# Turning the gated rows with VectorE and on-chip DMAs instead of TensorE in a Mamba-2 plus MoE-LoRA block

## The reference, cut to what matters

```python
g = y * jax.nn.silu(gate)                       # [tokens, 8192]
gg = g.reshape(b, s, G, INTER // G)             # 8 groups of 1024 channels
var = jnp.mean(gg * gg, axis=-1, keepdims=True)
gg = gg * jax.lax.rsqrt(var + EPS)
out = gg.reshape(b, s, INTER) * norm_w
return jnp.einsum('bsi,oi->bso', out, out_proj_w)   # [tokens, 512]
```

## Time and profile before

| what | value |
|---|---|
| time, median of 3 runs | 1656.18 us (1655.62 to 1657.89) |
| the profiled execution: time | 1656.76 us |
| the profiled execution: span of the trace | 1654.6 us |
| PE busy | 1616.8 us, 98% |
| DVE busy | 1367.3 us, 83% |
| POOL busy | 1341.1 us, 81% |
| ACT busy | 1232.1 us, 74% |
| granted TensorE clock, mean | 0.999 |

### The profile page before, as it was taken

How to read it: one execution, slowest core, us unless ns; L and a number is a source line. 1 busy time by engine, 2 the same in 40 slices (tenths; PEclk the granted TensorE clock), 3 DMA queues, 4 the chain that set the end, 5 groups by cost and what they waited for, 6 DMA issues and landing times.

```text
span 1654.6 us, 31655 instructions
## 1 busy us (share of the span) xinstructions
PE 1616.8 (98%) x10792; PEld 1300.1 (79%) x10792; DVE 1367.3 (83%) x1675; ACT 1232.1 (74%) x2625; POOL 1341.1 (81%) x1238
## 2 busy tenths in 40 slices
PE   7999999999999999999999999999999999999998
PEld 6777878878787877878778787887878787787776
DVE  5979788887979878788888888888788887879787
ACT  5267787777877777777877778687786877778775
POOL 3148689886998779897798968988698977989797
PEclk9999999999999999999999999999999999999999
DMA  3253366553644545454554535535454365544463
GB/s 129 68 190 112 101 186 178 152 155 109 197 127 123 151 154 163 112 149 128 166 176 116 157 115 166 164 115 164 125 183 125 115 170 141 158 127 146 127 164 104
DMA packets 216399, 236.09 MB, mean 143 GB/s; under 512 B 154280, under 2 KB 155824, under 8 KB 212016
## 3 DMA queue, kind: packets, MB, share of 16 engines
q1 hardware_dynamic: 216240, 234.08, 47.7%
HBM read 147.52 MB, written 55.05 MB: 122 GB/s over the span
## 4 chain that ended last, share of the span: by engine, by line
PE 65%; POOL 13%; ACT 8%; DVE 7%; issue 6%; DMA 0%; ACTq 0%; DVEq 0%; POOLq 0%; SPq 0%
PE P L261 8%; PE P L263 8%; PE P L262 8%; PE P L470 5%; PE P L480 5%; PE P L345 4%; PE P L487 4%; PE P L339 4%; PE P L338 4%; PE P L481 4%; ACT P L583 4%; PE P L495 3%; DVE hsX L790 2%; POOL xch L1115 2%; POOL AL L1090 2%
## 5 line engine op out<-in xcount | busy, mean ns | idle before, releaser
L583 ACT ACTIVATE P<-AB,SC 128x128 f32<-128x128 f32 x1016 | 305.9, 364 | 0.0
L261 PE MATMUL P<-xh,AH 128*128 128x512 f32 x656 | 267.8, 408 | 2.6 <-DVE xl L891 1.8
L790 DVE SCALAR_TENSOR_TENSOR hsX<-P,cwt,hsX 128x1023 f32<-128x1023 f32 x189 | 241.9, 1280 | 25.7 <-ACT hsX L520 21.2
L263 PE MATMUL P<-xh,AL 128*128 128x512 f32 x656 | 257.1, 392 | 0.0
L262 PE MATMUL P<-xl,AH 128*128 128x512 f32 x656 | 255.5, 389 | 0.0
L755 ACT ACTIVATE sq<-yb 128x512 bf16<-128x512 f32 x128 | 80.8, 631 | 212.6 <-DVE yb L1054 212.6
L1090 POOL TENSOR_TENSOR AL<-AR,AH 128x512 fp32r<-128x512 f32 x82 | 116.1, 1416 | 133.5 <-ACT AH L507 133.4
L480 PE MATMUL P<-OH,gTh 128*128 128x512 f32 x512 | 214.6, 419 | 2.5 <-DVE hsX L1070 1.5
L338 PE MATMUL P<-GH,xh 128*128 128x512 f32 x512 | 200.1, 391 | 0.2 <-ACT GH L552 0.2
L481 PE MATMUL P<-OH,gTl 128*128 128x512 f32 x512 | 200.3, 391 | 0.0
L339 PE MATMUL P<-GH,xl 128*128 128x512 f32 x512 | 199.6, 390 | 0.0
(11 more groups left out here) (214 smaller groups left out, 4144.2 us busy)
## 6 DMA issues: line engine op xcount, KB each, us to landing
AB<-acr_d SPq DMA_DIRECT2D x128, 512.0 KB, 4.6
half_d<-hsX SPq DMA_DIRECT2D x60, 512.0 KB, 3.3
AR<-in_wa SPq DMA_DIRECT2D x80, 256.0 KB, 2.8
TS<-in_wg SPq DMA_DIRECT2D x16, 1024.0 KB, 5.8
TS<-in_wo SPq DMA_DIRECT2D x16, 1024.0 KB, 4.8
part_d<-pl SPq DMA_DIRECT2D x64, 256.0 KB, 3.1
pl<-part_d SPq DMA_DIRECT2D x64, 256.0 KB, 3.2
SC<-sct_d SPq DMA_DIRECT2D x16, 128.0 KB, 5.3
```

What stands on the lines that cost most here:

```text
L261: te.matmul(o, ah_, bh_, start=(first and i == 0), stop=False)
L263: r = te.matmul(o, al_, bh_, start=False, stop=(last and i == n - 1))
L583: r = se.activation(decays(m)[:, h, :], AB[m % 2][:, h, :], ACT.Relu, bias=SC[s % 2][:, c, 3, h:h + 1], scale=-1.0)
L790: ve.scalar_tensor_tensor(out=o[:, d:T], in0=raw[:, 0:T - d], scalar=cwt[:, n, 3 - d:4 - d], in1=o[:, d:T], op0=ALU.mult, op1=ALU.add).the ...
```

## The change

The four PE transposes of each slot go (except in the last slot, which keeps them: `by_pe(j)` is true for `j == M - 1`). In their place:

- DVE turns the gated rows in 32x32 blocks with one `transpose` instruction (128x512) right after the gating, into a tile `blk`. It reads `yb` with a stride of 16 elements.
- SP moves the four bands of 32 partitions with four plain SBUF-to-SBUF DMAs (64 KB each) into `GTd[j % 2]`, a tile of 128 partitions. Partition `q` then holds channel `4q + k` in its part `k`; the host lays out the output weights and the norm weights to suit.
- ACT's `gTh` and DVE's `gTl` read `GTd` in SBUF, no longer bank 6 in PSUM. They are made one slot later, and the output product `O(j)` runs in slot `j + 2` instead of `j + 1` (`out_slot`); the products of slots 126 and 127 both come after slot 127.
- All that hangs on `O` moves one slot with it: ACT's copy or scaling of partial sums, DVE's alo, POOL's addition, SP's stores and loads. The splitting of the output weights moves from chunk 0 to chunk 1 on ACT (`OH`, except in segment 0) and for POOL's `OL`, and from chunk 1 to chunk 2 on DVE (`OL`); the next gate weights are loaded in chunk 3.
- Two groups of semaphores used in the preparation are merged to make room for the new ones.

```diff
+    def by_pe(j):
+        return j == M - 1
+
+    def out_slot(j):
+        return j + 1 if by_pe(j) else j + 2
+
+    outs_of = {m: [j for j in range(M) if out_slot(j) == m] for m in range(M + 2)}
...
-        if m:
-            jobs += [("O", m - 1, (4,))]
+        jobs += [("O", j, (4,)) for j in outs_of[m]]
...
-        if m < M:
+        if m < M and by_pe(m):
             jobs += [("GTr", m, (6,))]
...
+        gtd = sb("gtd", [128, 512])
...
+        blk, GTd = al[0], [al[1][:, :], gtd[:, :]]
...
+        def turned_rows(j):
+            if by_pe(j):
+                return bank("GTr", j).rearrange("p (k a i) -> p k a i", k=4, a=4)
+            return GTd[j % 2].rearrange("p (a k i) -> p k a i", a=4, k=4)
...
+                for j in outs_of[m + 1]:
+                    if by_pe(j):
+                        se.wait_ge(s_gtr, 1)
+                    else:
+                        se.wait_ge(gate_in[j % 2], 64 * (j // 2 + 1))
+                    if j:
+                        se.wait_ge(s_o, j)
+                    se.activation(by_block(gTh), turned_rows(j), ACT.Copy).then_inc(s_gth, 1)
...
-                    if c == 0:
+                    if c == (1 if s else 0):
                         se.wait_ge(s_ts3, s + 1)
                         se.wait_ge(ts_in, 16 * (3 + 2 * s))
...
-                    if c == 1:
+                    if c == out_c:
                         dve_output_lo(s, (1, 2))
...
                     ve.tensor_tensor(yb[:, :], bank("Y", m), tg[:, :], ALU.mult).then_inc(s_g, 1)
+                    if not by_pe(m):
+                        ve.wait_ge(s_g, m + 1)
+                        if m:
+                            ve.wait_ge(gate_in[(m - 1) % 2], 64 * ((m - 1) // 2 + 1))
+                        ve.transpose(blk[:, :].rearrange("p (b i) -> p b i", i=32),
+                                     yb[:, :].rearrange("p (j b) -> p b j", b=16)).then_inc(s_blk, 1)
...
-                if m < M:
-                    ve.wait_ge(s_gth, m + 1)
-                    ve.tensor_tensor(gTl[:, :, :], bank("GTr", m).rearrange("p (k t) -> p k t", k=4),
-                                     as_f(gTh[:, :, :]), ALU.subtract).then_inc(s_gtl, 1)
+                for j in outs_of[m + 1]:
+                    ve.wait_ge(s_gth, j + 1)
+                    ve.tensor_tensor(by_block(gTl), turned_rows(j), as_f(by_block(gTh)), ALU.subtract).then_inc(s_gtl, 1)
...
+        def sp_turn_rows(j):
+            sp.wait_ge(s_blk, j + 1)
+            if j >= 2:
+                sp.wait_ge(s_gtl, j - 1)
+            for a in range(4):
+                sp.dma_start(GTd[j % 2][:, a * 128:(a + 1) * 128], blk[32 * a:32 * a + 32, :]).then_inc(gate_in[j % 2], 16)
...
+                if m and not by_pe(m - 1):
+                    sp_turn_rows(m - 1)
```

147 lines of the change are left out of this document (81 added, 66 removed).

## The result

The changed kernel takes 1721.01 us (median of 4 runs, 1715.95 to 1727.43) against 1656.51 us (1655.62 to 1657.89) for the kernel before on the same chip: a ratio of 1.0391, 95% interval 1.0345 to 1.0436. It is slower by 64 us. The forecast was 1651 us, with a range from 1620 to 1684.

A forecast was written before the change was run, and what follows sets the result against it. PE, busy 98% of the span, was taken to pace the kernel; head -3, seven periods -10.5, last slots +5 and end +3 gave 1656.8 - 3 - 10.5 + 5 + 3 = 1651.3, so 1651 us, range 1620 to 1684.

The forecast's parts named there:

- the kinds of place named: New PE waits: B and C product for alo, first projection matmul for the convolution in chunk 3, Off for the gate.
- slots 120 to 126: Last seven slots, without projection work: 9.3 us each instead of 8.60 from added DVE and POOL work, +5 us.
- PE's loss of work: Four transposes leave PE's queue, 0.44 us a slot; with their waits 69 us if no other engine were late.
- The transpose, 0.67 us: DVE's new 128x512 block transpose in each of 127 slots, taken at 0.67 us, bounds 0.60 and 1.8.
- `gTl`, 1.25 us: DVE's gTl with both inputs in SBUF mostly meets POOL: 1.25 us, 0.57 more than now, and 0.45 more for POOL.
- The lateness, -1.5 us a period: Per 16 slots, PE's savings less DVE's lateness in three places: -1.5 us, over seven periods -10.5 us.
- the other ten slots keep the 0.44 us: Ten of 16 slots, outside the three late places, keep PE's 0.44 us each, and 0.2 us of waits together.
- Rival 4: DVE becomes the bound; beyond about 1.3 us added a slot, additions show, half size first: 1690 or 1665 us; chance 0.30.
- (b): Slot 50: OL moved to chunk 2 delays convolution, output product and gate; PE's distance behind the slot +2.9 us.
- (c): Slot 42: the same move, with four OH copies ahead of ACT's tap; PE's distance +0.2 us instead of -0.8.
- The end: After the last gating: the product of slot 126 now follows it and the last product waits for gTh, +3 us.
- The transfers, at nothing: The four DMAs a slot, 256 KB landing in 3.1 us, were costed at nothing.

The follow-up runs named there:

- experiment 1: Changed kernel with the block transpose reading 32 neighbouring columns of yb instead of every 16th: 1684.09 us (ratio 1.0169).
- experiment 7: OL operations cut to 32 of 512 columns: from the changed kernel 1710.83 us, from the contiguous, late transpose kernel 1652.81, from the kernel before 1646.49.
- experiment 5: Changed kernel with the transpose both reading neighbouring columns and placed at the end of DVE's slot, behind gTl: 1666.72 us (ratio 1.0052).
- experiment 6: Kernel before with one part added, result unused: strided DVE transpose alone 1684.52 us (1.0140); four SBUF DMAs a slot alone 1660.41 us (1.0018).
- experiment 8, first kernel: Changed kernel with the output product one slot behind instead of two, OL back in chunk 1: 2425.21 us.
- experiment 9: Contiguous, late transpose kernel with PE turning rows, ACT copying them, two slots' lag: some slots 1709.40 us; all slots 1753.20; all, gated rows stored in order, 1734.18.

## Why the prediction was wrong

Its direction was wrong, and its mechanism was right in kind: PE's gain came back as lateness of DVE, at the kinds of place named. Two of its steps failed, the price of the strided transpose (37 of the 70 us between 1651 and 1721) and the lateness that it let a given load cause (most of the other 33). By stretches of the trace (us more than before, forecast and measured; with the contiguous transpose of experiment 1, whose DVE load is below the forecast one, in the last column):

| stretch | forecast | measured | experiment 1 |
|---|---|---|---|
| up to slot 7 | -3 | +2.5 | +0.6 |
| slots 8 to 119, seven periods | -10.5 | +58.1 | +15.9 |
| slots 120 to 126 | +5 | +0.5 | +3.1 |
| from slot 127 to the end | +3 | +10.4 | +8.3 |

Step by step:

**PE's loss of work**, 0.44 us a slot, was right. Slot 52 is one that PE still paces; the stretch before and after:

```profile
760.71:775.08 14.37, 14.37 (x94) 11.80 (x93) 12.89 (x15) 10.69 (x23) 9.03 (x8) 1.00 0.48 132
```

```profile
787.54:801.46 13.92, 13.92 (x92) 11.36 (x91) 13.03 (x16) 11.18 (x25) 9.97 (x9) 1.00 0.68 173
```

Here 0.45 us of the change's promise arrived.

**The transpose, 0.67 us**, was mis-sized: 1.09. The nearest rows were of contiguous operands, and the stride stood in the diff. The upper bound, 1.8 us, covered it, but the value taken went by rows that do not have the stride. This term alone is worth 37 us (experiment 1).

**`gTl`, 1.25 us**, was mis-sized the other way: 0.88. That it is held by POOL is visible: at 682.85 (below) a POOL instruction had begun 0.08 us ahead of it and it takes 1.76 us; at 698.04 the POOL instruction in front of it had 0.24 us left and it takes 0.78. So POOL's share of 86% does not give the price, but how much of POOL's instruction is left; the medians are 0.93 us for one buffer and 0.69 for the other. The two errors almost cancel: DVE's load rose by 22.3 us a period (186.5 against 164.2), where 19.8 was forecast.

**The lateness, -1.5 us a period**, is the step that failed in the mechanism. With nearly the forecast load the period grew by 8.5 us. Experiment 1 shows it free of the transpose's price: DVE's sum in its 16 slots is 180.1 us, 15.9 more than before and 3.9 less than forecast, and they last 197.3 us, 1.8 more than before. So even a transpose of 0.71 us gives 1684. I had let lateness arise in three places and end there, while "the other ten slots keep the 0.44 us". Of the 16, apart from slot 49, which lost the `OL` work, six do (41 and 51 to 55); slot 44, for which nothing was forecast, alone takes 3.3 us more. DVE's timeline of slots 42 to 44 (start, us, engine, line) shows what happens instead:

```profile
665.24 1.11 DVE L1084 STREAM_TRANSPOSE al<-yb 128x512 f32<-128x512 f32 x1
...
669.34 1.78 DVE L871 TENSOR_TENSOR dxh<-hsX,SC 128x512 f32<-128x512 f32 x1
...
682.85 1.76 DVE L1114 TENSOR_TENSOR gTl<-al,gTh 128x512 fp32r<-128x512 f32 x1
684.54 1.77 DVE L871 TENSOR_TENSOR dxh<-hsX,SC 128x512 f32<-128x512 f32 x1
...
698.04 0.78 DVE L1114 TENSOR_TENSOR gTl<-gtd,gTh 128x512 fp32r<-128x512 f32 x1
```

Each slot hands its lateness to the next: the queue runs without a gap, the two `dxh` shown take 1.78 and 1.77 us, where the shortest takes 0.68, and three slots take 43.95 us for 43.53 us of DVE's work, where they took 39.95 for 33.70 before. Rival 4 had this mechanism, but with "half its size first": it put a transpose 0.6 us dearer at 1690 us, and one 0.42 us dearer gave 1721.

**(b) and (c), the move of `OL`,** forecast 2.9 us of lateness for slot 50. The slot does last 14.5 us instead of 11.75, 2.8 more, which looks as forecast, but with a transpose of another price in it, so that the agreement is partly luck. But `OL` had its price in chunk 1 already (experiment 7), which no wait showed in full.

**The end.** +3 us were forecast for the last product. Its start comes 9.5 us after the last PE transposes (1707.98 to 1717.49), where it was 2.1 us before (1646.52 to 1648.61), since the product of slot 126 now stands between them, waits for alo (1.28 us) and is followed by `gTh`, `gTl` and another wait (2.92 us). PE runs at half clock there, so that the last product itself takes 5.5 us instead of 3.0. The timeline of PE in the kernel after:

```profile
1707.98 0.72 PE L514 MATMUL P<-ident,yb 128*128 128x128 f32 x4 [0.54 <-DVE yb L1079]
1709.98 0.70 PE L499 MATMUL P<-OH,gTh 128*128 128x512 f32 x1 [1.28 <-DVE hsX L1103]
...
1717.49 0.79 PE L499 MATMUL P<-OH,gTh 128*128 128x512 f32 x1 [2.92 <-DVE hsX L1103]
...
1721.07 1.91 PE L506 MATMUL P<-OL,gTh 128*128 128x512 f32 x4
```

That is 7.4 + 2.5 = 10 us. The last seven slots came to 9.0 us each, 9.3 forecast, but the +5 us were not there: before, slots 120 to 126 had taken 8.9 us each in the mean (experiment 5), not the 8.60 of the one slot that was read.

**The transfers, at nothing,** were nearly right: 3 to 4 us (experiment 6).

**The sum of the runs.** From 1721: contiguous -37, late -17 more (1684.1 to 1666.7), and what is left over the kernel before is 8 to 10 us. In its profiled execution, 6.9 us slower by the spans, all of that and more lies behind slot 119 (12.5 us, experiment 5), where one more product follows the last gating; ahead of it the kernel gains 5.5 us. That this is so little, where 0.45 us of PE in each of 120 slots would be 54, is DVE again, idle for 0.25 us or less in seven of the 16 slots (42 and 50 among the stretches of experiment 5), together with 3 to 4 us for the DMAs and up to 4 for the move of `OL`. `gTl` from SBUF and the lag were not measured alone.

## What to carry to other kernels

Before moving work to a second engine, count its free time in front of each result that the first engine waits for; other free time, even in the same slot, is of no use. Here half of the average free time (15.7 of 31.3 us) was enough to lengthen the period (experiment 6). Place new work behind every result that another engine waits for (43 us here), and check the address pattern of an instruction against rows with the same pattern before taking a price from its shape. Price the end of the program too: a product that comes one slot later in a loop comes behind everything in the last slot (8.9 us in the best version).

## What was not expected of the hardware

**The granted clock fell inside the loop.** Before, the mean over 121.5 to 1648 us was 1.00. Now single stretches of the loop stand at half. Slot 45 has a mean clock of 0.87, its first 3.4 us one of 0.51 (of PE alone: length, busy and count, clock, DMA share, GB/s):

```profile
699.80:703.20 3.40, 3.40 (x37) 0.51 0.49 140
```

In the 10 us ahead of it PE had waited twice, as its timeline shows (wait and releaser in brackets), and after that the same matmul is listed with 0.63 us instead of 0.39:

```profile
693.37 0.50 PE L280 MATMUL P<-xh,AH 128*128 128x512 f32 x1 [1.33 <-DVE Cx L813]
...
698.18 0.50 PE L469 MATMUL P<-SH,CH 128*128 128x512 f32 x1 [1.79 <-DVE tg L847]
...
702.28 0.63 PE L500 MATMUL P<-OH,gTl 128*128 128x512 f32 x1
```

0.51 is the lower of the two levels, 1.2 GHz of 2.4. The mean clock of the profiled executions was 0.999 before, 0.985 after, 0.996 with the contiguous transpose, where PE's busy time is 17.3 us less for the same matmuls: 17.3 of the 43.6 us between these two spans. With waits in every slot (experiment 8, first kernel) it was 0.86. The four runs of the changed kernel say the same: 1715.95 and 1716.31 us at 0.994 and 0.993, 1725.71 and 1727.43 at 0.988 and 0.985. So waits of PE seem to cost more than their length. That is read from their order in time and from these means; no run changes the clock alone.

**A stride in a store costs as in a load**: the gating, 692 ns when it stores in order, took 1054 ns when it stored every 16th element (experiment 9).
